# Another order for a kernel's opening: W2's first two k tiles early, A3 behind W3's fourth block, Wr and B1 turned by VectorE

## The reference

```
x = x + x @ W0.T + 0.5 * (x @ A0[label0]) @ B0.T
x = x + x @ W_eff.T        # W1 + B1 @ A1 / 2, quantised by groups of 128 to a codebook, plus B1 @ A1 / 2
x = x + x @ W2.T + 0.5 * (x @ A2[label2]) @ B2.T
x = x + x @ W3.T + 2 * sum over experts e of gate_e * (x @ A3[e].T) @ B3[e].T
        # gates: softmax of the two largest of x @ Wr.T + 5 * one_hot(label7)
```

## Time and profile before

| | us |
|---|---|
| median of three executions | 594.64 |
| lowest and highest | 593.68, 594.65 |
| the profiled execution's own time | 594.47 |
| its span, first to last instruction | 592.7 |
| TensorE busy | 587.2 (99% of the span) |
| VectorE, ScalarE, GpSimd busy | 445.5, 235.2, 111.9 |

### The profile page before, as it was taken

How to read it: one execution, slowest core, us unless ns; L and a number is a source line. 1 busy time by engine, 2 the same in 40 slices (tenths; PEclk the granted TensorE clock), 3 DMA queues, 4 the chain that set the end, 5 groups by cost and what they waited for, 6 DMA issues and landing times.

```text
span 592.7 us, 9201 instructions
## 1 busy us (share of the span) xinstructions
PE 587.2 (99%) x3171; PEld 525.2 (89%) x3171; DVE 445.5 (75%) x804; ACT 235.2 (40%) x475; POOL 111.9 (19%) x131
## 2 busy tenths in 40 slices
PE   8999999999999999999999999999999999999998
PEld 7999999899999999999787888788888888888887
DVE  3498998999989855897788999957474747474744
ACT  3444233445432216544465477323233333333331
POOL 2101010003000000336324011041212121212110
PEclk9999999999999999999999999999999999999999
DMA  9962230164000000000333000223030303030301
GB/s 267 255 173 81 91 103 5 25 161 152 0 2 1 1 0 2 2 0 2 29 82 77 1 1 1 63 81 110 32 110 31 109 33 106 36 107 35 106 2 71
DMA packets 57826, 37.71 MB, mean 64 GB/s; under 512 B 26684, under 2 KB 51516, under 8 KB 57796
## 3 DMA queue, kind: packets, MB, share of 16 engines
q1 hardware_dynamic: 57796, 37.31, 22.6%
HBM read 28.91 MB, written 8.39 MB: 63 GB/s over the span
## 4 chain that ended last, share of the span: by engine, by line
PE 92%; DVE 6%; DMA 1%; issue 1%; ACT 1%; POOL 0%; DVEq 0%; ACTq 0%; POOLq 0%
PE acc L1789 39%; PE acc L1671 34%; PE aux L1789 5%; PE acc L1910 4%; PE aux L1661 3%; PE acc L1912 2%; PE aux L1747 1%; PE acc L1918 1%; PE acc L1919 1%; PE acc L1661 1%; DVE g_lo L1390 1%; PE acc L1827 1%; PE acc L1829 1%; DMA g<-in_L_cond_W_dram 1%; DVE t_lo L1363 1%
## 5 line engine op out<-in xcount | busy, mean ns | idle before, releaser
L1789 PE MATMUL acc<-b_hi,g_lo 128*128 128x512 f32 (+1 forms) x266 | 89.0, 389 | 0.1
L1671 PE MATMUL acc<-hg_hi,w_hi 128*128 128x352 f32 (+2 forms) x384 | 87.3, 335 | 0.6 <-DVE w_lo L1103 0.6
L1789 PE MATMUL acc<-t_hi,g_lo 128*128 128x512 f32 x256 | 87.4, 400 | 0.0
L1671 PE MATMUL acc<-hg_lo,w_hi 128*128 128x352 f32 (+2 forms) x384 | 86.0, 331 | 0.0
L1671 PE MATMUL acc<-hg_hi,w_lo 128*128 128x352 f32 (+2 forms) x384 | 85.8, 331 | 0.0
L610 POOL TENSOR_TENSOR xr<-xr 128x512 f32<-128x512 f32 x32 | 41.2, 1309 | 143.4 <-DVE g_lo L1390 141.9
L1671 PEld LDWEIGHTS acc<-hg_hi,w_hi 128*128 128x128 f32 x384 | 66.4, 188 | 1.8 <-DVE w_lo L1103 0.8
L1671 PEld LDWEIGHTS acc<-hg_hi,w_lo 128*128 128x128 f32 x384 | 67.3, 188 | 0.0
L1671 PEld LDWEIGHTS acc<-hg_lo,w_hi 128*128 128x128 f32 x384 | 67.3, 188 | 0.0
L1199 DVE TENSOR_TENSOR q<-q,qtmp 128x1024 f32<-128x1024 f32 x48 | 59.5, 1240 | 1.7
L1789 PEld LDWEIGHTS acc<-b_hi,g_lo 128*128 128x128 f32 x266 | 49.6, 188 | 11.2 <-DVE part L1561 0.5
(11 more groups left out here) (279 smaller groups left out, 1119.0 us busy)
## 6 DMA issues: line engine op xcount, KB each, us to landing
out_dram<-part SPq DMA_DIRECT2D x31, 256.0 KB, 2.8
x_st<-in_x_dram SPq DMA_DIRECT2D x60, 128.0 KB, 2.9
g<-in_L_cond_W_dram SPq DMA_DIRECT2D x8, 512.0 KB, 7.1
w_st<-in_L_cond_W_dram SPq DMA_DIRECT2D x8, 512.0 KB, 5.1
a_t<-in_L_cond_weight_dram SPq DMA_DIRECT2D x8, 512.0 KB, 5.7
w_raw<-in_L_cond_weight_dram SPq DMA_DIRECT2D x8, 512.0 KB, 4.2
a_raw<-in_L_cond_lora_A_dram SPq DMA_DIRECT2D x5, 128.0 KB, 3.4
a_raw<-in_L_cond_lora_A_dram SPq DMA_DIRECT2D x20, 32.0 KB, 2.0
```

What stands on the lines that cost most here:

```text
L1671: last = pe.matmul(acc[0:a.shape[-1], slot, bank * BANK:bank * BANK + c1 - c0], a[:, k, :], b[:, k, c0:c1], start=(at == 0 and n == 0), st ...
L1789: last = pe.matmul(dst, p, q, start=start and n == 0, stop=stop and n == 2, skip_group_check=True)
```

## The change

W2's block 0 is loaded in two parts: its first two k tiles (128 KB) behind W3's block 0, the other six behind W3's block 1. The first products start from the two tiles. Wr is loaded in four pieces into an area that VectorE zeroes first, and VectorE transposes it in 32 x 32 squares; TensorE's eight transposes of it are gone. A3 is loaded behind W3's block 3 and transposed between k tiles 2 and 3. B1 is loaded in four pieces of 32 columns, in runs of 128 bytes, between W3's blocks 5 and 6, and two VectorE transposes turn it; TensorE's eight are gone. A1 is loaded before W2's block 1, where it was behind it. `BRIDGE` is 5. W3's splits are done in halves for k below 4. Bank 2 of k tiles 0 to 3 is done together. `turn_w3` transposes the tile with the unit matrix last.

```diff
             for k in range(KT):
                 sp.dma_start(g[:, :, k * P:(k + 1) * P], slices(W3)[:, :, k * P:(k + 1) * P]).then_inc(w3_in[k], 16)
                 if k == 0:
-                    load_w2(0)
+                    sp.dma_start(w_st[:, 0, 0:2], slices(W2)[:, 0:2, 0:P]).then_inc(first_in, 16)
                 if k == 1:
+                    sp.dma_start(w_st[:, 0, 2:KT], slices(W2)[:, 2:KT, 0:P]).then_inc(w_in[0], 16)
+                    sp.wait_ge(wr_clear, 1)
+                    for a in range(QUARTERS):
+                        sp.dma_start(wr_st[a * Q:a * Q + E],
+                                     Wr.rearrange("e (k a q) -> a e k q", a=QUARTERS, q=Q)[a]).then_inc(wr_in, 16)
+                if k == 3:
                     sp.dma_start(a3_st, A3.rearrange("e r d -> (e r) d")).then_inc(a3_in, 16)
-                    sp.dma_start(wr_st, Wr).then_inc(a3_in, 16)
+                if k == 5:
+                    for a in range(QUARTERS):
+                        sp.dma_start(b1_st[a * Q:(a + 1) * Q].rearrange("r (c q) -> r c q", q=Q),
+                                     B1.rearrange("(c r) (h q) -> h r c q", r=Q, q=Q)[a % 2]).then_inc(b1_in, 16)
+            for u in range(2):
+                sp.dma_start(row(3, slice(u * R1, (u + 1) * R1)), A1).then_inc(lora_in, 16)
             load_w2(1)
...
-            for u in range(2):
-                sp.dma_start(b1_dup[:, :, u], B1.rearrange("(k p) r -> p k r", p=P)).then_inc(lora_in, 16)
-                sp.dma_start(row(3, slice(u * R1, (u + 1) * R1)), A1).then_inc(lora_in, 16)
...
+            act.wait_ge(w_eye, 1)
+            act.copy(w_hi[:, 0, 0:2], w_st[:, 0, 0:2]).then_inc(first_hi, 1)
             for k in range(KT):
                 act.wait_ge(w3_t, k + 1)
-                act.copy(hg_hi[:, k, 0:D], w3_at(k)).then_inc(split_hi, 1)
+                if k < 4:
+                    act.copy(hg_hi[:, k, 0:HD], w3_at(k)[:, 0:HD]).then_inc(half_hi, 1)
+                    act.copy(hg_hi[:, k, HD:D], w3_at(k)[:, HD:D]).then_inc(split_hi, 1)
+                else:
+                    act.copy(hg_hi[:, k, 0:D], w3_at(k)).then_inc(split_hi, 1)
...
+            dve.memset(wr_st[:], 0.0).then_inc(wr_clear, 1)
...
+                if k in (5, 6):
+                    if k == 5:
+                        dve.wait_ge(b1_in, 16 * QUARTERS)
+                    cols = slice((k - 5) * HD, (k - 4) * HD)
+                    dve.transpose(b1_tr[:, cols].bitcast(U32), b1_st[:, cols].bitcast(U32)).then_inc(b1_t, 1)
...
             def turn_w3(k):
-                pe.wait_ge(w3_eye, k + 1)
+                pe.wait_ge(w3_in[k], 16)
                 if k >= 2:
                     pe.wait_ge(h_ready, k - 1)
-                for n in range(KT):
+                for n in [n for n in range(KT) if n != k] + [k]:
+                    if n == k:
+                        pe.wait_ge(w3_eye, k + 1)
...
             turn_w3(1)
-            pe.wait_ge(w_split, 1)
-            tile_of(0, 0, 0, 0, three_pairs(0, 0), (0, 1))
-            pe.wait_ge(a3_in, 32)
-            turn_a3((0, 1))
-            turn_w3(2)
-            tile_of(0, 1, 1, 0, three_pairs(0, 0), (0, 1))
+            first_tile(0)
+            first_tile(1)
+            turn_w3(2)
+            turn_w3(3)
+            first_tile(2)
+            pe.wait_ge(a3_in, 16)
+            turn_a3((0, 1))
+            first_tile(3)
+            turn_w3(4)
             pe.wait_ge(a3_done, 2)
             turn_a3((2,))
-            for k in range(2):
+            pe.wait_ge(wr_done, 1)
+            for k in range(4):
                 tile_of(0, k, k, 0, three_pairs(0, 0), (2,))
-            for k in range(2, KT):
+            for k in range(4, KT):
                 if k + 1 < KT:
                     turn_w3(k + 1)
                 if k == a3_tiles[2][0]:
                     pe.wait_ge(a3_done, 3)
-                if k == KT - 1:
-
-                    pe.wait_ge(lora_in, 64)
-                    pe.wait_ge(h_ready, KT - 1)
-                    for n in range(KT):
-                        last = turn_tile(aux[:, n * P:(n + 1) * P], b1_dup[:, n].rearrange("p u r -> p (u r)"))
-                    last.then_inc(b1_t, 1)
                 tile_of(0, k, k, 0, three_pairs(0, 0))
```

More of the change, by code:

```diff
@@ L290, in row @@
             return a_t[rows, n, 0:width]
-        a3_st, wr_st, b1_st, b2_st, a1_st = row(6), row(7, slice(0, E)), row(5), row(4, width=KT * R), row(3)
-        b1_dup = b1_st.rearrange("p (k u r) -> p k u r", k=KT, u=2)
+        a3_st, b1_st, b2_st, a1_st = row(6), row(5), row(4, width=KT * R), row(3)
+        wr_st, wr_tr = place("wr_st", 37120, [P, KT, Q]), place("wr_tr", 37120 + 4 * KT * Q, [P, KT, Q])
+        b1_tr = place("b1_tr", 133888, [P, D])
         b2_raw = b2_st.rearrange("p (k r) -> p k r", k=KT)
@@ L480, in _ @@
             load_w2(5)
-            sp.wait_ge(b1_t, 1)
+            sp.wait_ge(b1_t, 2)
             load_w1(5)
@@ L1106, in w2_low @@
                 w_low(t, w_st[:, t % 2], t + 1)
+            dve.memset(wr_st[:], 0.0).then_inc(wr_clear, 1)
+            dve.wait_ge(first_hi, 1)
+            dve.tensor_tensor(w_lo[:, 0, 0:2], w_st[:, 0, 0:2], w_hi[:, 0, 0:2].bitcast(F32),
+                              ALU.subtract).then_inc(first_lo, 1)
             for k in range(KT):
+                if k < 4:
+                    dve.wait_ge(half_hi, k + 1)
+                    dve.tensor_tensor(hg_lo[:, k, 0:HD], w3_at(k)[:, 0:HD], hg_hi[:, k, 0:HD].bitcast(F32), ALU.subtract)
+                c0 = HD if k < 4 else 0
@@ L1109, in _ @@
                 dve.wait_ge(split_hi, k + 1)
-                dve.tensor_tensor(hg_lo[:, k, 0:D], w3_at(k), hg_hi[:, k, 0:D].bitcast(F32),
+                dve.tensor_tensor(hg_lo[:, k, c0:D], w3_at(k)[:, c0:D], hg_hi[:, k, c0:D].bitcast(F32),
                                   ALU.subtract).then_inc(h_ready, 1)
-                if k == 0:
-                    w2_low(0)
-                if k in (1, 2):
-                    for bank in ((0, 1), (2,))[k - 1]:
+                if k == 1:
+                    w_low(0, w_st[:, 0, 2:KT], 1, w_lo[:, 0, 2:KT], w_hi[:, 0, 2:KT])
+                    dve.wait_ge(wr_in, 16 * QUARTERS)
+                    dve.transpose(wr_tr[:].rearrange("p k q -> p (k q)").bitcast(U32),
+                                  wr_st[:].rearrange("p k q -> p (k q)").bitcast(U32)).then_inc(wr_t, 1)
@@ L1684, in turn_w3, with first_tile @@
             def turn_w3(k):
-                pe.wait_ge(w3_eye, k + 1)
+                pe.wait_ge(w3_in[k], 16)
                 if k >= 2:
                     pe.wait_ge(h_ready, k - 1)
-                for n in range(KT):
+                for n in [n for n in range(KT) if n != k] + [k]:
+                    if n == k:
+                        pe.wait_ge(w3_eye, k + 1)
                     last = turn_tile(w3_at(k)[:, n * P:(n + 1) * P], g[:, n, k * P:(k + 1) * P])
                 last.then_inc(w3_t, 1)
+            def first_tile(k):
+                for n, (a, b) in enumerate(((w_hi, hg_hi), (w_lo, hg_hi), (w_hi, hg_lo))):
+                    if n == 0:
+                        pe.wait_ge(split_hi, k + 1)
+                    elif n == 1:
+                        pe.wait_ge(first_lo, 1)
+                        if k >= 2:
+                            pe.wait_ge(w_split, 1)
+                    else:
+                        pe.wait_ge(h_ready, k + 1)
+                    for bank in range(2):
+                        c0, c1 = thirds(C_LOW2)[bank]
+                        pe.matmul(acc[:, 0, bank * BANK:bank * BANK + c1 - c0], a[:, 0, k, :], b[:, k, c0:c1],
+                                  start=(k == 0 and n == 0), stop=False, skip_group_check=True)
             pe.wait_ge(made, 2)
@@ L1697, in turn_a3 @@
             def turn_a3(tiles):
-                for c0, c1, st in ((0, ER, a3_st), (ER, NR, wr_st)):
-                    for bank in tiles:
-                        k0, k1 = a3_tiles[bank]
-                        for k in range(k0, k1):
-                            last = turn_tile(a3_at(bank, k0, k1)[:, k - k0, c0:c1], st[:, k * P:(k + 1) * P])
+                for bank in tiles:
+                    k0, k1 = a3_tiles[bank]
+                    for k in range(k0, k1):
+                        last = turn_tile(a3_at(bank, k0, k1)[:, k - k0, 0:ER], a3_st[:, k * P:(k + 1) * P])
                 last.then_inc(a3_t, 1)
```

46 lines of the change are left out of this document (31 added, 15 removed).

## The result

The changed kernel takes 597.29 us (median of 6 runs, 596.21 to 598.34); the kernel before, in the same session, 594.63 (593.68 to 594.76). The ratio is 1.0045, with an interval of 1.0035 to 1.0055: slower by 2.7 us, where the prediction had 0.5 us faster, and outside its range, which ended at 595.8. The profiled execution took 598.34 us with a span of 596.6. It is the longest of the six, 1.0 us over their median, so its single figures stand at the slow end.

What follows compares the result with a forecast made beforehand. TensorE was taken as the bound, with the start of `delta(0)` deciding. W2's block 1 at 28.05 plus 5.2 gave 33.25 against 33.77, 0.5 us earlier: 594.1 us. Range 592.5 to 595.8, the forecast's own 593.7 to 594.6.

Steps and rivals of the forecast that it cites:

- a forecast of one moment: Start of `delta(0)`, at 33.77 us before: its shift was taken to set the change of the whole time.
- The 5.2 us from W2's block to `delta(0)`: Opening: GpSimd's addition 0.47, ScalarE's w_hi 1.05, w_lo to `delta(0)` 3.57, hand-overs about 0.1.
- The 42.5 us for the second `delta`: Pass 1's second `delta` needed only near 42.5 us (five k tiles of 1.6 after 35), so later loads are covered.
- the sum of the loads: Opening's DMA queue: B1's 3.3 us and A1's 1.4 us move W2's block 1 from 23.35 to 28.05.
- B1's 3.3: B1's load ahead of W3's block 6, priced as 524 KB at A2's 161 GB/s: 3.3 us.
- Rival 3: B1's load: pieces of 32 partitions and half rows hold the queue longer, up to 6.8 us, 597.6; chance 0.11 past 1.2 us.
- its point of 28.6: Landing of W2's block 1 from which the slower case decides, with B1 at 3.8 us (138 GB/s).
- Rival 1: Opening's loads lighter than counted: W2's block by 27, gain 1.5 to 2.1 us, 592.5 to 593.1; chance 0.29 over 1.2 us.
- Rival 2: Nothing arrives at `delta(0)`: TensorE's 2.3 us spent waiting, loads 0.5 us dearer, 594.6; chance 0.58 together with the forecast.
- Rival 4: Opening: TensorE's slow issue pace lasts longer, each us costing 0.5 us, price beyond cover about 0.5 us; chance 0.02.
- Behind it nothing waits: After `delta(0)`: TensorE has no waits, so any gain in the opening is kept and any delay paid in full.
- the other leg: W3's blocks 6 and 7 to `delta(0)`: ends at 31.6 us, a floor 2.1 us better than before.

Runs made afterwards that it cites:

- e2: Changed kernel with B1's four pieces replaced, in the same place, by four A2 loads of the same 128-byte runs over 128 partitions: 596.53 us.
- e6: Changed kernel with Wr's four small loads replaced by one load of the same bytes: 596.03 us.
- e8: Changed kernel with A1 loaded behind W2's block 1 instead of ahead of it, B1's pieces left in place: 596.05 us.
- e10: Kernel before with B1 (256-byte runs) and A1 both loaded between W3's blocks 5 and 6: 596.36 us.
- e11: Kernel before with only B1's two loads (256-byte runs) moved between W3's blocks 5 and 6: 594.27 us.
- e12: Kernel before with only A1's two loads moved between W3's blocks 5 and 6: 593.99 us.
- v1_wr_act: Changed kernel with Wr issued by ScalarE, B1 and A1 loaded behind W2's block 1, TensorE transposing B1 behind k tile 7, `delta(0)` one k tile later: 594.85 us.
- e4: Changed kernel with Wr's four small loads issued behind W3's block 2 instead of ahead of it: 597.25 us.
- e5: Changed kernel with 30 more unit-matrix transposes on TensorE while it waits for W3's block 6: 596.92 us.
- e3: Changed kernel with B1 loaded in the same place as two loads of 256-byte runs over 128 partitions: 595.43 us.
- e1: Changed kernel with B1's four pieces issued behind W2's block 1 and VectorE's two transposes behind a_lo: 596.89 us.
- e7: Changed kernel with B1 and A1 as before: loaded behind scale, B1 in 256-byte runs and transposed by TensorE ahead of k tile 7: 595.20 us.
- v2: Changed kernel with Wr in one load, A1 then B1 (256-byte runs) behind W2's block 1, TensorE transposing Wr and B1, `delta(0)` one k tile later: 595.48 us.
- e9_dve_extra: Kernel before with one more VectorE addition of 1.23 us, its result unused, behind bst: 595.37 us.
- v3_tables: New front, B1 and A1 behind W2's block 1, book and scale behind W3's block 4, 18 VectorE table steps moved into its gaps: 595.26 us.

## Why the prediction was wrong

**Right.** "The forecast is therefore a forecast of one moment": in after and in e2 to e6, e8, e10, e11 and e12 the shift of `delta(0)` against 33.77 and that of the execution agree within 0.3 us (after 3.87 and 3.87, e8 0.12 and 0.1, e11 -0.58 and -0.6). The 5.2 us from W2's block to `delta(0)`, ScalarE's w_hi released through GpSimd's addition, the loads deciding and not TensorE, the first product (8.69 against 8.3), the transposes on VectorE in gaps (0.70 and 0.71 us), all held. (The 42.5 us for the second `delta` are 43 by the prediction's own sum, and 42.77 in the kernel before; nothing hangs on it.)

**The step that failed** is the sum of the loads, "W2's block 1 moves from 23.35 to 23.35 + 3.3 + 1.4 = 28.05", and in it above all B1's 3.3. The block came at 32.41, 4.36 us later than that. The lateness arises in three stretches:

- Up to W3's block 5, 1.1 us. "Up to W3's block 4 the bytes are the same as now ... so that block lands as now" left out that the four loads of Wr are four instructions of the queue: 3.16 us, where the kernel before issues Wr once in 0.38, and a hole of 157 GB/s at 7 to 8 us. (The wait for `wr_clear` did cost nothing.) How much of the 1.1 us is theirs is open: block 5 is at 17.76 in e6_wr_one and at 17.80 in v1_wr_act, which lack the hole.
- From block 5 to block 7, 3.1 us. This stretch has B1 in it and no A1. It takes 4.22 us before and 10.60 after, so B1 cost 6.4 us here, not 3.3. In the other five kernels with B1 in 128-byte runs or A2 in its place it is 3.0 (e4), 3.2 (e8), 5.1 (e2), 5.2 (e6) and 5.6 (e5); in 256-byte runs 4.9 (e3) and 3.1 (e11). In the four kernels without it (e1, e7, v1, v2) the stretch differs from before by -0.9 to +0.8.
- From block 7 to W2's block 1, 0.2 us. A1 cost 1.6 us here, and 1.4 to 2.9 in e1 to e6, where 1.4 was forecast.

So the price was read as bytes over the rate of a window (524/161), and the delay of the block behind was larger. B1's windows moved 127 to 156 GB/s, which makes some 3.8 us (an estimate, at 139, their mean with the 140 of the fourth us). Most of the rest is an engine that falls behind. The instruction fetch took one engine from 19.28 to 20.82 us, in the middle of B1's load, 1.5 us (1.15 before). B1's packets of 128 bytes start at 960 to 1094 a us from 17 to 20, and the last 93 take from 21.0 to 22.3, about the pace of one engine. That the same engine was still late at W2's block fits, but the rows don't number the engines, so it is not shown. Nor is it shown why the delay is 3.0 us in some kernels and 6.4 in others.

It is not shown either that the two loads cost more together than their sum. From block 5 to W2's block 1, e10_place takes 5.7 us more than before, e11_b1_only 3.2 and e12_a1_only 1.5. But v2_order, which has nothing new ahead of this block and A1 right behind it, takes 2.8 more, and v1_wr_act 0.9 less. So these sums can't be told from the scatter, and a rival stays untested: loads queued behind a block may delay it too. What the runs do show is that both loads in this place make the kernel before 2.0 us slower, and either alone does not.

**Rival 3** is nearest to what happened: W2's block came behind its point of 28.6, B1 cost 6.4 us where it reckoned with up to 6.8, and the time is near its 597.6. But it put the price on B1's pieces of 32 partitions, and e2_a2_runs shows that those cost what A2's form costs. It was given 0.11, because B1's term was taken from a window of another stretch of the kernel, and the delay of the slowest engine was counted once, at 1.1 us as before. The range therefore ended 1.5 us short. **Rival 1**, a lighter stream, with a chance of 0.29, had the strongest case against it in the rows of A2 and falls: no kernel with B1 ahead of W2's block brought that block before 26.29, and none with A1 there too before 28.83. **Rival 2** differs only in size. **Rival 4** did not occur in the opening, but another form of it did: "No row here shows a clock below 1.00" was true of before and was read as if waits of 2 to 3 us could not change it. In after that is covered (e5_fill), in e1_b1_behind and e7_front it costs 1.7 us, and untraced executions of the kernel before have lower mean clocks too (0.997 and 0.994).

**"Behind it nothing waits"**, so that "whatever is gained in the opening is kept", was too wide. The kernel before's own rows have short waits of TensorE's weight loads for VectorE between 359 and 402 us, which the prediction passed over:

```profile
PEld acc L1918 <- DVE g_lo L1525: 0.8, 2, 0.5
...
PEld aux L1661 <- DVE v_sb L1507: 0.6, 1, 0.6
```

And TensorE waits for nobody at 143 us only as long as VectorE is shifted by the same amount. e9_dve_extra, v1_wr_act, v2_order and v3_tables show this second bound behind the first. Had the loads been free, the gain might have been a few tenths, not the 2.1 us of the other leg; that is an estimate from these runs, and no run has free loads.

Under the kernel before are only e11_b1_only (594.27, an interval that holds 1) and e12_a1_only, 593.99, ratio 0.9983 [0.9967, 0.9998]; neither takes anything of the new front. The 0.6 us of the latter are less than the 1.2 us that the prediction named as told apart from nothing.

## What to carry to other kernels

When a load is moved ahead of one that others wait for, its price is the delay of the block behind it, not its bytes over the rate of a window in which it runs elsewhere: B1 was forecast at 3.3 us and cost 3.0 to 6.4. Look also at the number of DMA instructions in front (four of 8 KB opened a hole in the stream), and find the point at which the cover ends (block 6 at 22.5 was free, at 25.5 it came with a loss of 2 us). Trace more than one execution, or several kernels with the same loads, before a landing time is explained to the tenth. Try each moved load alone in the old kernel; that separated the place from the rest of the change in three runs. Before a gain at the front is counted as kept, look for the second engine: delay it by one instruction and see if the end moves.

## What the runs showed of the hardware

- A single wait of TensorE of 2.5 to 3.3 us was met by a stretch in which the granted clock was 0.50, the 1.2 GHz level: 26.4 to 29.8 in after, 35.4 to 38.8 in e1_b1_behind, 29.2 to 32.6 in e7_front. Waits of 2.3 us (e10_place) and 2.0 us (e2_a2_runs) were not, in the executions profiled. Other executions of e7_front, five of ten, had none. The price is 1.7 us where nothing covers it. The Trainium skill, in "TensorE: Matmul & The Clock Gate", section "Part 1: The HAM clock gate", says that the array is throttled again after idling; by that page the new waits themselves speak against the change, and these rows agree.
- A block of 512 KB lands with its slowest engine: 19 GB/s for 1.5 us at the end of W2's block 1, with one engine's 64 packets left. e8_a1_behind shows a like hole, 83 GB/s from 20 to 22 us.
- One instruction fetch of 16 KB held one DMA engine for 1.15 us in before (between 16 and 20 us) and 1.5 us in after (19.3 to 20.8), in the middle of the loads.
- Four loads of 8 rows with 128-byte runs, 8 KB each, took 3.16 to 5.00 us of SyncE's queue (after, e4_wr_behind), and the stream behind them fell to 157 and 77 GB/s. One load of the same 32 KB on 32 rows took 1.13 us (e6_wr_one), and the stream stayed at 301. The time on the queue is not all their own: issues also wait there, as when six blocks of W3 take 10.36 us in the kernel before.
